# VectorE's attend step in a new order, GpSimd's product behind VectorE's, and the second token list's one-hots two columns a step

## The reference

```
score = jnp.einsum('bci,bcj->bij', k, q) / math.sqrt(l)
score = jax.nn.softmax(score, axis=0)          # over the BATCH, not over j
out = jnp.einsum('bci,bij->bcj', v, score)     # q = layernorm(x), k = v = ctx

logits = jnp.einsum('th,eh->te', x, router_w)
topk_logits, topk_idx = jax.lax.top_k(logits, 2)
probs = jax.nn.softmax(topk_logits, axis=-1)
hmid = gelu(jnp.einsum('th,efh->etf', x, w1) + b1)
y = jnp.einsum('etf,ehf->eth', hmid, w2) + b2
out = jnp.einsum('eth,te->th', y, combine)
```

## Time and profile before

| what | value |
|---|---|
| median of three timed executions | 800.47 us (797.47 to 800.8) |
| profiled execution, its time | 802.11 us |
| profiled execution, its span | 800.3 us |
| attend, from the first product to the last store's issue | about 155 to 296 us of the span |
| token lists and routing | about 295 to 323 us |
| experts, two rounds | about 323 us to the end |
| TensorE busy | 715.2 us, 89% of the span |
| VectorE busy | 611.1 us, 76% |
| GpSimd busy | 539.4 us, 67% |
| ScalarE busy | 404.7 us, 51% |
| mean granted TensorE clock | 0.945 of full speed |

### The profile page before, as it was taken

The page is one execution under the profiler, slowest core; times in us unless marked ns, Lnnn a source line. Parts: engine busy times, 40 slices in busy tenths (PEclk is TensorE's granted clock), DMA queues, the critical chain, the costliest instruction groups (busy, mean ns, idle before and its releaser), DMA issues. The chain is left out here.

```text
span 800.3 us, 21890 instructions
## 1 busy us (share of the span) xinstructions
PE 715.2 (89%) x5691; PEld 610.8 (76%) x5692; DVE 611.1 (76%) x1482; ACT 404.7 (51%) x754; POOL 539.4 (67%) x665
## 2 busy tenths in 40 slices
PE   6997788699999955599999999999978999999995
PEld 4665555487777755399999999998957999999994
DVE  5998799889999978787777777727466677676764
ACT  3888677457666762154444444414433545444441
POOL 5775577778888840647777777754777777777763
PEclk9999899899999965599999999979999999999998
DMA  7884543148887750436555555542354444444440
GB/s 224 251 252 144 182 131 121 36 133 254 263 263 263 253 205 35 133 110 194 178 186 186 186 165 157 194 140 92 101 159 140 135 124 149 121 147 125 146 126 29
DMA packets 72927, 128.71 MB, mean 161 GB/s; under 512 B 9243, under 2 KB 46116, under 8 KB 72752
## 3 DMA queue, kind: packets, MB, share of 16 engines
q0 software_dynamic: 22528, 68.06, 27.9%
q1 hardware_dynamic: 50352, 60.07, 23.2%
HBM read 85.61 MB, written 47.24 MB: 166 GB/s over the span
## 5 line engine op out<-in xcount | busy, mean ns | idle before, releaser
L1054 ACT ACTIVATE work<-psum,b1T 128x256 f32<-128x256 f32 x304 | 127.8, 471 | 254.6 <-PE psum L682 254.6
L682 PE MATMUL psum<-work,w1T_high 128*128 128x256 f16 x1216 | 208.0, 276 | 2.5 <-ACT work L1062 2.5
L705 PE MATMUL psum<-w2T_high,slots 128*128 x1216 | 206.5, 275 | 0.8 <-issue 0.8
L682 PE MATMUL psum<-work,w1T_low 128*128 128x256 f16 x608 | 168.0, 276 | 0.0
L705 PE MATMUL psum<-w2T_low,slots 128*128 x608 | 167.2, 275 | 0.0
L682 PEld LDWEIGHTS psum<-work,w1T_high 128*128 x1216 | 120.3, 99 | 18.1 <-issue 3.0
L940 DVE CAST slots<-work 128x512 f16<-128x512 f32 x152 | 67.2, 442 | 84.3 <-ACT work L1054 81.8
L705 PEld LDWEIGHTS psum<-w2T_high,slots 128*128 128x128 f16 x1216 | 116.8, 99 | 14.4 <-issue 1.3
L531 POOL DMA_INDIRECT slots<-rows_first,slots x84 | 85.7, 1021 | 55.4 <-issue 52.3
L538 POOL DMA_INDIRECT rows_second<-slots x76 | 82.3, 1082 | 55.6 <-issue 31.3
L942 DVE TENSOR_TENSOR slots<-work,slots 128x512 f16<-128x512 f32 x152 | 106.5, 701 | 5.2
(11 more groups left out here) (126 smaller groups left out, 1179.5 us busy)
## 6 DMA issues: line engine op xcount, KB each, us to landing
rows_first<-slots SPq DMA_DIRECT2D x32, 520.0 KB, 3.0
work<-in_ctx SPq DMA_DIRECT2D x64, 256.0 KB, 3.3
slots<-in_x SPq DMA_DIRECT2D x32, 256.0 KB, 3.5
work<-in_x SPq DMA_DIRECT2D x32, 256.0 KB, 3.0
work<-in_L_ffn_w SPq DMA_DIRECT2D x32, 256.0 KB, 2.8
slots<-rows_first,slots POOLq DMA_INDIRECT x84, 3.6
rows_second<-slots POOLq DMA_INDIRECT x76
slots<-rows_second,slots POOLq DMA_INDIRECT x76, 3.5
```

Of the source, the lines that this page charges most:

```text
L682: mm = pe.matmul(h, w1T[pw][:, f, c, bass.ds(e * P, P)], xT[r2][:, (px * HC + c) * GROUP:(px * HC + c + 1) * GROUP], start=(c == 0 and px ...
L705: mm = pe.matmul(y, act16[r2][pa][:, f * GROUP + s * P:f * GROUP + (s + 1) * P], w2T[pw][:, f, bass.ds(e * DIM, DIM)], start=(f == 0 and p ...
L1054: last = act.activation(act32[r2][:, f * GROUP:(f + 1) * GROUP], psum[:, 2 + 2 * r2 + f // 2, (f % 2) * GROUP:(f % 2 + 1) * GROUP], ACT.Ge ...
```

## The change

There are three parts. (1) In attend, VectorE's pieces are written in a new order, in two parts: first `low`, `below`, the probabilities, the denominator, the copy of the experts' numbers and the product; then the sum with x, the reciprocal, the index search, the statistics, the maxima and the mean. For this `below` moves to lag 7, the denominator to 8, the probabilities to 9 and the store to 10. (2) GpSimd's product of a pair waits for VectorE's product of the same pair, and GpSimd's `norm` moves from lag 2 to lag 3. (3) The second list's one-hots are no longer made in expert steps 0 to 3, 16 batches each, but in steps 4 to 35, two batches each, and each batch's columns lie side by side.

```diff
+        LIST_FROM = LIST_STEP - BATCH // 2
...
-        L_CT, L_PV, L_XN, L_LOWX, L_XNT, L_LG, L_P = 1, 2, 4, 5, 5, 6, 7
-        L_XL, L_STORE = 1, 8
+        L_CT, L_PV, L_NM, L_XN, L_LOWX, L_XNT, L_LG, L_BL, L_P, L_CB = 1, 2, 3, 4, 5, 5, 6, 7, 8, 9
+        L_XL, L_STORE = 1, 10
...
                 if live(i, k, 0, PAIRS):
                     m = i + k
+                    pool.wait_ge(a_probv, m + 1)
                     pool.tensor_tensor(slot2(m * 2, 0, PROD_POOL), slot2(m * 2, 0, PROD_POOL),
...
-                if live(i, k, L_PV, PAIRS):
-                    norm(a_mean, i + k - L_PV, (k - L_PV) % RING, a_pstep, a_norm)
-            pipeline(pool, PAIRS, RING, 2 * RING, L_PV, attend)
+                if live(i, k, L_NM, PAIRS):
+                    norm(a_mean, i + k - L_NM, (k - L_NM) % RING, a_pstep, a_norm)
+            pipeline(pool, PAIRS, RING, 2 * RING, L_NM, attend)
...
                 for b in range(BATCH):
-                    q = b // w
-                    if b % w == 0:
-                        pe.wait_ge(r_lane, 4 * rnd + q + 1)
-                        pe.wait_ge(r_tiles, 4 * rnd + q + 1)
-                    mm = pe.matmul(psum[:, LIST_BANK[rnd], 0:TILES], lanes[:, :, b], tiles[:, :, b], start=(b == 0), stop=(b == BATCH - 1))
+                    if rnd:
+                        lane, tile = lane_hot[:, b * P:(b + 1) * P], tile_hot[:, b * TILES:(b + 1) * TILES]
+                        if b == 0:
+                            pe.wait_ge(r_lane, 4 + BATCH // 2)
+                            pe.wait_ge(r_tiles, 4 + BATCH // 2)
...
+            def one_hots_of_second(j):
+
+                b = BATCH + j * 2
+                one, two = tile_one[:, bass.ds(j * 2 * TILES, 2 * TILES)], tile_hot[:, bass.ds(j * 2 * TILES, 2 * TILES)]
+                as_tiles, as_lanes = "p (b n) -> p b n", "p (b l) -> p b l"
+                dve.tensor_tensor(one.rearrange(as_tiles, b=2), tile_of[:, bass.ds(b, 2)].unsqueeze(2).to_broadcast([P, 2, TILES]),
+                                  iota16[:, 0:TILES].unsqueeze(1).to_broadcast([P, 2, TILES]), ALU.is_equal).then_inc(r_ones, 1)
+                dve.tensor_tensor(lane_hot[:, bass.ds(j * 2 * P, 2 * P)].rearrange(as_lanes, b=2), lane_of[:, bass.ds(b, 2)].unsqueeze(2).to_broadcast([P, 2, P]),
+                                  iota16.unsqueeze(1).to_broadcast([P, 2, P]), ALU.is_equal).then_inc(r_lane, 1)
+                dve.wait_ge(r_ones, j + 5)
+                dve.tensor_tensor(two.rearrange(as_tiles, b=2), one.rearrange(as_tiles, b=2), mark[:, bass.ds(j * 2, 2)].unsqueeze(2).to_broadcast([P, 2, TILES]),
+                                  ALU.mult).then_inc(r_tiles, 1)
...
-                if isinstance(i, int) and i + k < 4:
-                    one_hots(1, i + k)
+                if rnd == 0 or (isinstance(i, int) and LIST_FROM <= i + k < LIST_STEP):
+                    one_hots_of_second(i + k - LIST_FROM)
```

More of the change, by code:

```diff
@@ L656, in list_tokens @@
             def list_tokens(rnd):
-                tiles = tile_hot.rearrange("p (n b) -> p n b", b=BATCH)
-                lanes = lane_hot.rearrange("p (l b) -> p l b", b=BATCH)
-                w = BATCH // 4
                 for b in range(BATCH):
-                    q = b // w
-                    if b % w == 0:
-                        pe.wait_ge(r_lane, 4 * rnd + q + 1)
-                        pe.wait_ge(r_tiles, 4 * rnd + q + 1)
-                    mm = pe.matmul(psum[:, LIST_BANK[rnd], 0:TILES], lanes[:, :, b], tiles[:, :, b], start=(b == 0), stop=(b == BATCH - 1))
+                    if rnd:
[3 more added lines that the diff above has]
+                            pe.wait_ge(r_tiles, 4 + BATCH // 2)
+                    else:
+                        lane, tile = lane_hot.rearrange("p (l b) -> p l b", b=BATCH)[:, :, b], tile_hot.rearrange("p (n b) -> p n b", b=BATCH)[:, :, b]
+                        if b % 16 == 0:
+                            pe.wait_ge(r_lane, b // 16 + 1)
+                            pe.wait_ge(r_tiles, b // 16 + 1)
+                    mm = pe.matmul(psum[:, LIST_BANK[rnd], 0:TILES], lane, tile, start=(b == 0), stop=(b == BATCH - 1))
                 mm.then_inc(r_list, 1)
@@ L780, in attend @@
                     dve.tensor_scalar(den[:, r2, :], exps[:, r2, :, 1, 1], WSCALE, WSCALE, ALU.mult, ALU.add).then_inc(a_den, 1)
-                if live(i, k, L_LG, PAIRS):
-                    m, r2 = i + k - L_LG, (k - L_LG) % 2
-                    wait_apart(dve, a_ranked, m + 1)
-                    for j in range(2):
-                        last = dve.max(ranked[:, r2, j, 1, :], ranked[:, r2, j, 0, :])
-                    last.then_inc(a_top, 1)
+                    dve.wait_ge(a_topi, m + 1)
+                    dve.tensor_copy(choice[:, :, bass.ds(m * 2, 2)], topi[:, r2, :, 0:ROUNDS].rearrange("p b r -> p r b")).then_inc(a_choice, 1)
+                if live(i, k, 0, PAIRS):
+                    m = i + k
+                    dve.tensor_tensor(slot2(m * 2, PROD_POOL, 2 * DIM - PROD_POOL), slot2(m * 2, PROD_POOL, 2 * DIM - PROD_POOL),
+                                      ssum[:, PROD_POOL:].unsqueeze(1).to_broadcast([P, 2, 2 * DIM - PROD_POOL]), ALU.mult).then_inc(a_probv, 1)
                 if live(i, k, L_PV, PAIRS):
@@ L795, in attend @@
                     dve.reciprocal(inv[:, r2, :], den[:, r2, :]).then_inc(a_inv, 1)
[L796 to L800 removed]
+                if live(i, k, L_BL, PAIRS):
+                    m, r2 = i + k - L_BL, (k - L_BL) % 2
                     for j in range(2):
@@ L809, in attend @@
                     last.then_inc(a_stat, 1)
-                if live(i, k, L_P, PAIRS):
-                    m, r2 = i + k - L_P, (k - L_P) % 2
-                    dve.wait_ge(a_inv, m + 1)
-                    dve.tensor_tensor(slot2(m * 2, PR, EXPERTS), exps[:, r2, :, 0, :], inv[:, r2, :].unsqueeze(2).to_broadcast([P, 2, EXPERTS]),
-                                      ALU.mult).then_inc(a_comb, 1)
                 if live(i, k, L_LG, PAIRS):
                     m, r2 = i + k - L_LG, (k - L_LG) % 2
-                    dve.wait_ge(a_topi, m + 1)
-                    dve.tensor_copy(choice[:, :, bass.ds(m * 2, 2)], topi[:, r2, :, 0:ROUNDS].rearrange("p b r -> p r b")).then_inc(a_choice, 1)
+                    wait_apart(dve, a_ranked, m + 1)
+                    for j in range(2):
+                        last = dve.max(ranked[:, r2, j, 1, :], ranked[:, r2, j, 0, :])
+                    last.then_inc(a_top, 1)
                 if live(i, k, L_PV, PAIRS):
@@ L824, in attend @@
                     last.then_inc(a_mean, 1)
[L825 to L829 removed]
+            pipeline(dve, PAIRS, RING, 3 * RING, L_CB, attend)
             steps = [0]
@@ L1031, in attend @@
                     act.activation(exps[:, r2].rearrange("p j t e -> p (j t e)"), below[:, r2].rearrange("p j t e -> p (j t e)"), ACT.Exp).then_inc(a_exps, 1)
-            pipeline(act, PAIRS, RING, 2 * RING, L_LG, attend)
+            pipeline(act, PAIRS, RING, 2 * RING, L_BL, attend)
             for r in range(RING):
```

24 lines of the change are left out of this document (12 added, 12 removed).

## The result

The changed kernel takes 806.04 us (median of 11 runs, 801.04 to 812.3), the kernel before 800.76 (11 runs beside them, 796.39 to 802.7). The ratio is 1.0082 with an interval of 1.0048 to 1.0117. The profiled execution took 805.22 us with a span of 803.4.

What follows compares the result with a forecast made beforehand. Bounds: in attend a circle of GpSimd and VectorE waits, in the experts TensorE. Terms -5.0 + 0.5 - 2.3 - 9.5 = -16.3 us gave 784.2 against the median; own range 781 to 788, 8 in 10 from 778 to 791.

Steps and rivals of the forecast that it cites:

- The held product: Attend: VectorE's probabilities, held until GpSimd's product is done, would take 0.15 us instead of 0.90, freeing 0.75 a step.
- the circle: Attend: waits over three steps from VectorE's sum through GpSimd, norm, ScalarE and TensorE; 11.44 us, 3.81 a step.
- What closes next: Attend: the part naming the next bound, not VectorE's 3.24 us but 3.81 a step, with TensorE's 3.67 as floor.
- VectorE, sum to the product's end: Attend: VectorE's step without held time, 3.24 us, and its product's tail, taken as 3.3.
- handoffs: Attend: five passes of work between engines, estimated at 0.1 us each, 0.5 in sum.
- From the first to the last sum: Attend, 28 steps: a gain of 0.18 us a step, -5.0 us, with -2.5 and -9 as alternatives.
- Start: Attend's start: TensorE's first L635 late by up to a GpSimd product, mostly taken back; +0.5 us (0 to 1.6).
- End: Attend's end: pair 27's store goes out later, so the iota holds no denominator; -2.3 us (0 to -3.7).
- The list: Experts, second list on TensorE: 64 matmuls in 3.6 us for 10.64, no low clock after; -9.5 us.
- The one-hots: Expert steps: three added VectorE instructions a step, 1.05 us, hidden in 1.34 us free; worth 0.
- The upper bound: Expert steps: the added VectorE instructions at 1.56 us a step would cost 7.0 us, about half of it hidden.
- attend gains nothing: Rival for attend, chance 0.13: norm stretched by another 0.3 us, 12.0 over three steps, 4.0 a step; time 791.5.

Runs made afterwards that it cites:

- attend alone: The changed kernel with the old second list and its old one-hots, so only attend differs from the kernel before: 814.47 us, ratio 1.0154.
- the list alone: The kernel before with only the second list and its one-hots changed, attend as before: 789.3 us, ratio 0.9838.
- the kernel at 1.57: The kernel before with the new second list, but its matmuls' 76 moving columns 64 elements apart: 800.38 us, ratio 1.0005.

## Why the prediction was wrong

**The held product: right.** L790 takes 0.17 us for 0.90. With the circle open, VectorE's new order and lags give 3.70 to 3.72 a step in the mean, for 3.90 before.

**The circle: right mechanism, a term mis-sized.** This is the step that failed, "What closes next". I added 11.44 us; the circle of the rows above is 12.48. By its parts:

| part | forecast | measured |
|---|---|---|
| VectorE, sum to the product's end | 3.3 | 4.10 |
| GpSimd's product | 1.54 | 1.54 |
| norm | 1.8 | 1.59 |
| ScalarE | 1.09 | 1.09 |
| TensorE | 3.21 | 3.36 |
| handoffs | 0.5 | 0.80 |

The last row is 0.20, 0.09, 0.21, 0.06 and 0.24 us. The largest error is VectorE's: I took its step without waits, 3.24, but in front of `low` (L781) it stands still for 0.59 us. I take this for the arithmetic of addresses; the profile says only `issue`. Before, no such gap shows: there VectorE is held shortly before, and the two may have overlapped, which no run shows. It is that long once in a turn of the loop and 0.14 in the next step (from 220.60 to 220.74). That gap is no row of busy time and so wasn't in a sum of busy times. The circle in the table has VectorE's part near its longest and norm's at its shortest. Over the 23 circles VectorE's is 3.7 in the mean and norm's 1.9, from 1.6 to 2.6, so the term of 3.3 is the one most off there too.

**The clock: not in the prediction.** I had forecast that engines would idle in the circle, and hadn't asked what TensorE's clock does then. Before, TensorE was busy 88.25 of 96 us, with a gap of 0.32 in a step. The closed circle gives it idle stretches of 0.2 to 2.4 us. The two longest were each followed by the low clock, and those two steps are 4.8 and 2.7 us over the mean of the others: 7.5 us in one execution. Not all of that is the clock's. In the longer step TensorE's work from L619 to the end of L637 takes 6.2 us (240.91 to 247.14) for 3.36, so 2.9 of the 4.8; in the other L619 and L637 take 1.4 us more than at 1.00. The rest is the idle time itself. That long steps go when the wait is filled was shown by the run; why the engines fall so far apart at these places is open. The price by steps is read from one trace, and I take the scatter of 801 to 812 us as theirs, without having shown it. The longest execution of attend alone, with six low stretches, fits that.

The Trainium skill (TensorE: Matmul & The Clock Gate, section HAM oscillation — how this bites in real kernels) describes this pattern: TensorE starved again and again, and its clock going down and up again. The trace agrees as to the pattern, with 0.50 behind the 2.14 us gap; the waits in that section's example, about 3 to 5 us, are longer than any here.

**From the first to the last sum** I forecast -5.0; it is +9.1 (130.05 for 120.97). 7.5 of the 14.1 us between are the two long steps, the rest is mostly the longer circle: without the first three steps, which fill the pipeline, and the longest one, the other 27 have a mean of 4.08 for the 3.81 of the forecast. That is also over the 3.99 of before, so attend would have lost a little without any low clock.

**Start: right within its range.** The first sum is 1.3 us later; +0.5 was said, with a bound of 1.6. The room later in the circle that should take it back doesn't show.

**End: wrong.** I forecast -2.3 and it is +3.3. I argued that the store of pair 27 goes out two steps later, so that the iota falls behind the last denominator. The store did go out later, but so did the denominators: they have lag 8 for 7. The iota, at 11.15 us behind the last sum for 6.57, holds one of them for 3.63 us as before, and the drain is a step longer besides. I had moved one side of a race and left the other.

**The list: right, its size a little more.** -9.5 was said. 10.64 became 2.50 us, 0.039 a matmul, and the clock holds, in the list and behind it: 8.1 + 2.5 = 10.6 us. I took the f16 transposes as the nearest row, 0.056, but these move 128 columns and a matmul of the list 76; by the columns it is 0.033. The Trainium skill (SBUF — State Buffer, section Door 1: The DMA port swizzle, its note on cachelines) says that SBUF has lines of 16 bytes, that each access which crosses to a new line pays a penalty, and that one can stride for free by 8 elements of bf16. The columns here, f16 of the same size, lay 64 apart. The runs agree as to the kind, with 2.50 to 10.64 us for the list, and VectorE's writing shows the same, 0.42 to 1.30.

**The one-hots: right.** 1.04 us a step for a forecast of 1.05, and hidden: with the list alone TensorE is full. The upper bound, 1.56 a step, was priced at half of 7.0 us; the kernel at 1.57 loses 2.0.

**The rivals.** The one nearest to what happened is "attend gains nothing", 12.0 us for the circle. It had the size almost right (12.4 in the mean), but its time, 791.5, left out the clock and the end. None of my cases let attend lose: I bounded a step below by engines' own times and above by 4.0, the time of before, for no reason that a row gave.

## What to carry to other kernels

A wait added between two engines has to be followed round every circle that it closes, and the circle has to be summed with address gaps and handoffs in it, not with busy times alone; then divide by its steps and compare with the fullest engine. Here a lag and a wait were each free, and together cost 18 to 19 us. If the sum is near an engine's own step, ask what TensorE's clock will do in the idle pieces, since a circle that starves it can cost twice; and when a lag moves an end, move the waits on both sides of the race. An f16 operand of TensorE like these one-hots is best laid out with its columns side by side, and written so as well.

## What was not expected of the hardware

- More work made the kernel faster: some 0.2 us of extra transposes a step, 7.5 us less in all. The long idle stretches went, and TensorE's clock stayed at 1.00 from 185 to 265 us.
- Behind an idle stretch of TensorE of 2.14 us its granted clock was 0.50; behind one of 2.40 us in the kernel with the list alone, where TensorE otherwise had no long waits, it stayed 1.00; and in attend alone it fell behind stretches from 0.98 us on.
- Of a matmul with 128 weight columns and 76 moving ones in f16, columns 64 elements apart cost 0.131 us when it is the moving side, 0.089 the weights, 0.166 both, and 0.039 neither. With columns apart the pace was the same at a granted clock of 1.00 and of 0.50, and the clock fell while these matmuls ran.
- VectorE's one-hot of 256 f16 elements takes 0.42 us written side by side and 1.30 with 64 elements between.
